# One list of work per engine and row, with the output projection split, in a cross-attention and mixture-of-experts kernel

## The reference

```python
x = x + attention(layernorm(x), ctx)      # x, ctx: 8 rows of the batch x 128 tokens x 256
x = x + moe(layernorm(x))

def attention(x, h_ctx_kv):               # 16 query heads, 4 key/value heads, width 128
    q = rms_norm(x @ wq, q_norm_w); k = rms_norm(x @ wk, k_norm_w); v = x @ wv
    k_ctx = rms_norm(h_ctx_kv @ wk_ctx, k_norm_w); v_ctx = h_ctx_kv @ wv_ctx
    q = q * cos + rotate_half(q) * sin;  k = k * cos + rotate_half(k) * sin
    # each key head serves 4 query heads: a group
    scores = q @ concat(k_ctx, k).T / sqrt(128) + causal mask on the second half
    out = softmax(scores) @ concat(v_ctx, v)
    return out.reshape(8, 128, 2048) @ wo

def moe(xt):                              # sigmoid router, best 2 of 8 experts, plus a shared expert
    ...
```

## Time and profile before

| | |
|---|---|
| median of 3 runs | 354.92 us (354.77 to 354.96) |
| the profiled execution | 355.51 us, of which span of the core 353.8 us |
| TensorE busy (PE) | 323.0 us, 91% |
| VectorE busy (DVE) | 313.5 us, 89% |
| ScalarE busy (ACT) | 260.5 us, 74% |
| GpSimd busy (POOL) | 170.0 us, 48% |
| granted TensorE clock | 0.999 of full speed |

### The profile page before, as it was taken

One profiled execution on the slowest core, in us unless ns is written; L12 is line 12 of the kernel. 1 busy time (PEld: TensorE's weight loads), 2 busy tenths in 40 slices (PEclk: granted clock), 3 DMA queues, 4 the chain that ended last, 5 costly groups with the idle time before them and its releaser, 6 DMA issues.

```text
span 353.8 us, 7342 instructions
## 1 busy us (share of the span) xinstructions
PE 323.0 (91%) x2242; PEld 218.4 (62%) x2242; DVE 313.5 (89%) x602; ACT 260.5 (74%) x910; POOL 170.0 (48%) x247
## 2 busy tenths in 40 slices
PE   6868878899999999999999999999999999999994
PEld 6444545476667666766676667666766677756452
DVE  1789999999999899989998999899989998866763
ACT  3786889766987698769866986798679756847641
POOL 4866648663754275428541744174417420072620
PEclk9999999999999999999999999999999999999999
DMA  7887200012034003500310002000100000055783
GB/s 235 318 265 238 48 0 0 3 30 17 1 114 98 11 0 110 109 4 0 59 44 0 0 0 44 0 0 0 30 0 0 3 2 0 2 99 99 131 156 111
DMA packets 42450, 21.07 MB, mean 60 GB/s; under 512 B 31672, under 2 KB 39872, under 8 KB 42432
## 3 DMA queue, kind: packets, MB, share of 16 engines
q1 hardware_dynamic: 41712, 20.60, 23.3%
q10 hardware_dynamic: 720, 0.26, 0.4%
HBM read 12.20 MB, written 1.05 MB: 37 GB/s over the span
## 4 chain that ended last, share of the span: by engine, by line
PE 35%; DVE 25%; ACT 19%; issue 11%; POOL 4%; DMA 3%; DVEq 1%; SPq 0%; ACTq 0%; POOLq 0%
PE proj L1400 10%; ACT probs L568 8%; DVE probs L1014 6%; PE pt_ps L1363 6%; DVE nmax L1002 4%; PE turn L1309 3%; PE o_ps L1373 3%; DVE pT_lo L940 3%; PE sc_ps L1330 3%; PE proj L1215 3%; ACT pT_hi L469 2%; POOL q_rot L799 2%; DVE q_t L931 2%; DMA wq<-in_L_xattn_wq_dram 2%; ACT q_junk L512 2%
## 5 line engine op out<-in xcount | busy, mean ns | idle before, releaser
L568 ACT ACTIVATE probs<-sc_ps,nbias,q_r 128x256 f32<-128x256 f32 x128 | 70.9, 571 | 4.3 <-DVE nbias L1006 3.8
L799 POOL TENSOR_TENSOR q_rot<-q_t 128x512 f32<-128x512 f32 x32 | 41.4, 1294 | 42.2 <-DVE q_t L933 41.4
L1014 DVE TENSOR_SCALAR probs<-probs,rden 128x256 f32<-128x256 f32 x128 | 51.8, 466 | 1.1
L512 ACT ACTIVATE q_junk<-proj 128x128 bf16<-128x128 f32 x128 | 34.1, 297 | 11.3 <-DVE q_t L933 11.2
L469 ACT ACTIVATE pT_hi<-pt_ps 128x512 f16<-128x512 f32 x64 | 34.8, 597 | 10.1 <-PE pt_ps L1363 10.1
L940 DVE SCALAR_TENSOR_TENSOR pT_lo<-pt_ps,pT_hi 128x512 f16<-128x512 f32 x64 | 41.0, 681 | 0.1
L1002 DVE TENSOR_REDUCE nmax<-sc_ps 128x4 f32<-128x1024 f32 x32 | 38.9, 1215 | 1.5 <-PE sc_ps L1352 1.5
L1215 PE MATMUL proj<-wq_hi,xT 128*128 128x512 f16 x128 | 38.1, 379 | 0.0
L1363 PE MATMUL pt_ps<-ident,probs 128*128 128x128 f32 x256 | 33.3, 273 | 0.8 <-DVE probs L1014 0.6
L753 POOL TENSOR_TENSOR q_r<-q_me,power 128x4 f32<-128x4 f32 x32 | 32.5, 1014 | 2.5
L469 ACT ACTIVATE qT_hi<-turn 128x512 f16<-128x512 f32 x32 | 19.4, 607 | 18.1 <-PE turn L1309 18.1
(11 more groups left out here) (216 smaller groups left out, 866.9 us busy)
## 6 DMA issues: line engine op xcount, KB each, us to landing
wq<-in_L_xattn_wq_dram SPq DMA_DIRECT2D x4, 512.0 KB, 7.6
w<-in_L_ffn_w_dram SPq DMA_DIRECT2D x2, 1024.0 KB, 11.0
wq<-in_L_xattn_wo_dram SPq DMA_DIRECT2D x1, 2048.0 KB, 8.2
ctx_b<-in_ctx_dram SPq DMA_DIRECT2D x8, 128.0 KB, 2.3
out_dram<-x_all SPq DMA_DIRECT2D x4, 256.0 KB, 2.2
x_all<-in_x_dram SPq DMA_DIRECT2D x1, 896.0 KB, 14.1
wkc<-in_L_xattn_wk_ctx_dram SPq DMA_DIRECT2D x1, 512.0 KB, 4.3
wk<-in_L_xattn_wk_dram SPq DMA_DIRECT2D x1, 512.0 KB, 5.2
```

The lines of the kernel that those rows point to most:

```text
L512: last = nc.scalar.activation(junk[:, head], bank[:, head], ACT.Square, scale=scale, accum_out=dst[:, h:h + 1])
L568: last = nc.scalar.activation(probs[:, h, :], sc_ps[:, h, :], ACT.Exp, bias=nbias[:, h:h + 1], scale=q_r[:, g, h:h + 1], accum_out=den[:, ...
L799: nc.gpsimd.tensor_tensor(q_rot[:], q_t1[:], q_t2[:], ALU.add).then_inc(q_added, 1)
L1014: last = nc.vector.tensor_scalar(probs[:, h, :], probs[:, h, :], rden[:, h:h + 1], None, ALU.mult)
```

## The change

The loops over `g` go. Each engine's `row` becomes a written list, and the orders are new:

- TensorE: in stage 0 the projection of group 2 stands behind the turn of group 1 and ahead of `turn_probs`. `out_proj` is split: groups 0 and 1 right after `scores(b, 1)` and ahead of the turn of group 2, groups 2 and 3 after the projection of group 3. The next row's group 0 is turned in stage 3, and `kc_turn` comes last.
- ScalarE: `p_copy` of a group ends its list rather than beginning the next one. The next row's `q_copy` of group 0 and `k_copy` come ahead of group 3's exponentials, `kc_copy` between their two halves (`exps` has a parameter `half`).
- VectorE: the maximum and `nbias` are two steps now (`scores_max`, `scores_bias`), and so are `rden` and the products with it (`sums`, `normalise` with a list of heads), with other work between the heads.
- POOL: `ln_root` stands first. Rows 1 to 6 are all written out, and the casts are eight pieces of half the size for each weight, spread over two rows. SyncE waits for these after rows 2, 4 and 6.
- `ctx_high` waits for `vc_proj` in row 1's case only. The last row and what follows it keep their steps.

The lists, in the order ScalarE, POOL, VectorE, TensorE. What stands under `if first:` and the lines that go are left out.

```diff
             def row(b, first, last):
+                u = G * b
+                exps(b, 0, 0)
+                exps(b, 0, 1)
+                if not first and not last:
+                    ctx_high(b + 1)
+                q_squares(b, 2)
+                if not first:
+                    o_copy(u - 1, 3)
+                vc_copy(b)
+                v_copy(b)
...
+                q_copy(b, 2)
+                if not last:
+                    ln_high(b + 1)
+                p_copy(u)
+                exps(b, 1, 0)
+                exps(b, 1, 1)
+                q_squares(b, 3)
+                o_copy(u, 0)
...
+                q_copy(b, 3)
+                p_copy(u + 1)
+                exps(b, 2, 0)
+                exps(b, 2, 1)
+                if not last:
+                    kc_squares(b + 1)
+                    q_squares(b + 1, 0)
+                    k_squares(b + 1)
+                o_copy(u + 1, 1)
+                if not last:
+                    kc_scale(b + 1)
+                if last:
+                    act.wait_ge(t_sh2, 1)
+                    copy(gateT[:].rearrange("p c e -> p (c e)"), proj[0][:, D:D + DC * E])
+                    copy(sh2T[:], proj[0][:, 0:D]).then_inc(r_sh2, 1)
+                    xn_copy(1)
...
+                p_copy(u + 2)
+                if not last:
+                    q_copy(b + 1, 0)
+                    k_copy(b + 1)
+                exps(b, 3, 0)
+                if not last:
+                    kc_copy(b + 1)
+                exps(b, 3, 1)
...
+                if not last:
+                    q_squares(b + 1, 1)
+                    q_copy(b + 1, 1)
+                    o_copy(u + 2, 2)
+                    p_copy(u + 3)
...
             def row(b, first, last, cast=None):
+                if not first and isinstance(b, int) and b == 1:
+                    wo_rest(1)
+                if cast:
+                    cast(0)
+                    cast(1)
+                if not last:
+                    ln_root(b + 1)
+                q_add(b, 2)
+                q_roots(b, 2)
+                if not last:
+                    ln_low(b + 1)
+                q_add(b, 3)
+                q_roots(b, 3)
...
+                if not first:
+                    l2_root(b - 1)
+                if cast:
+                    cast(2)
+                    cast(3)
+                if last:
+                    return
+                q_add(b + 1, 0)
+                kc_roots(b + 1)
+                k_roots(b + 1)
+                k_scale(b + 1)
+                q_roots(b + 1, 0)
...
+                q_add(b + 1, 1)
+                q_roots(b + 1, 1)
...
+            for b, start in ((1, 0), (2, 4)):
+                row(b, False, False, cast_to(w1_b, w1_32, d_w1, w1_cast, start))
+            for b, start in ((3, 0), (4, 4)):
+                row(b, False, False, cast_to(w3_b, w1_32, d_w3, w3_cast, start))
+            for b, start in ((5, 0), (6, 4)):
+                row(b, False, False, cast_to(w2_b, w2_32, d_w2, w2_cast, start))
...
+            def scores_bias(b, g):
+                u = G * b + g
                 dve.wait_ge(s_max, u + 1)
                 dve.wait_ge(q_root, u + 1)
                 seen(dve, s_exp, u)
                 nc.vector.tensor_tensor(nbias[:], nmax[:], q_r[:, g, :], ALU.mult).then_inc(s_bias, 1)
+            def sums(b, g):
                 u = G * b + g
                 dve.wait_ge(s_exp, u + 1)
                 nc.vector.reciprocal(rden[:], den[:]).then_inc(s_rden, 1)
+            def normalise(b, g, heads=range(R)):
+                dve.wait_ge(s_rden, G * b + g + 1)
+                for h in heads:
                     last = nc.vector.tensor_scalar(probs[:, h, :], probs[:, h, :], rden[:, h:h + 1], None, ALU.mult)
+                    if h == R - 1:
+                        last.then_inc(s_probs, 1)
...
             def row(b, first, last):
+                scores_max(b, 0)
...
+                q_low(b, 1)
+                if not first:
+                    o_low(u - 2, 2)
+                    scores_bias(b, 0)
+                    p_low(u - 1)
+                q_turn(b, 2)
+                sums(b, 0)
+                normalise(b, 0, (0,))
+                if not last:
+                    ln_stats(b + 1)
+                    dve.wait_ge(ln_stat, b + 2)
+                normalise(b, 0, (1,))
+                if not last:
+                    ln_gather(b + 1)
+                if not last and not first:
+                    ctx_low(b + 1)
+                normalise(b, 0, (2, 3))
+                vc_low(b)
+                v_low(b)
...
+                if not last:
+                    ln_scale(b + 1)
+                scores_max(b, 1)
+                scores_bias(b, 1)
+                q_low(b, 2)
+                if not first:
+                    o_low(u - 1, 3)
+                p_low(u)
+                q_turn(b, 3)
+                sums(b, 1)
+                normalise(b, 1, (0,))
+                if not first:
+                    residual(b - 1)
+                normalise(b, 1, (1, 2, 3))
...
+                o_low(u, 0)
+                scores_max(b, 2)
+                q_low(b, 3)
+                scores_bias(b, 2)
+                if not first:
+                    second_norm(b - 1)
+                p_low(u + 1)
+                if last:
+                    xn_copy(0)
+                else:
+                    q_turn(b + 1, 0)
+                sums(b, 2)
+                normalise(b, 2, (0,))
+                if not last:
+                    k_turn(b + 1)
+                normalise(b, 2, (1, 2, 3))
+                if not last:
+                    k_add(b + 1)
+                scores_max(b, 3)
+                o_low(u + 1, 1)
+                p_low(u + 2)
+                scores_bias(b, 3)
...
+                if not last:
+                    q_low(b + 1, 0)
+                    k_low(b + 1)
+                    q_turn(b + 1, 1)
+                    kc_low(b + 1)
+                sums(b, 3)
+                normalise(b, 3)
...
+                if last:
+                    o_low(u + 2, 2)
...
             def row(b, first, last):
+                scores(b, 0)
+                q_turn(b, 1)
...
+                q(b, 2)
+                if not first:
+                    turn_probs(u - 1)
+                vc(b)
...
+                v(b)
+                if not first:
+                    mix(u - 1, 3)
+                scores(b, 1)
+                if not first:
+                    out_proj(b - 1, (0, 1))
+                q_turn(b, 2)
+                turn_probs(u)
...
+                q(b, 3)
+                if not first:
+                    out_proj(b - 1, (2,))
+                    out_proj(b - 1, (3,))
+                mix(u, 0)
+                scores(b, 2)
+                q_turn(b, 3)
+                turn_probs(u + 1)
+                if not last:
+                    q(b + 1, 0)
+                    kc(b + 1)
+                    k(b + 1)
+                if last:
+                    turn_down_gate()
+                    turn_xn2(0, (q_sq, G * B))
+                    turn_xn2(1, (q_ready, G * B))
+                mix(u + 1, 1)
+                scores(b, 3)
+                turn_probs(u + 2)
+                if not last:
+                    q(b + 1, 1)
+                    q_turn(b + 1, 0)
+                    k_turn(b + 1)
+                if last:
+                    pe.wait_ge(r_sh2, 1)
+                    logits(0)
+                    turn_shared()
+                mix(u + 2, 2)
+                if not last:
+                    kc_turn(b + 1)
```

More of the change, by code:

```diff
@@ L557, in v_copy, with exps @@
                 copy(v_hi[:, 1, :], turn[:], V_SCALE / XW).then_inc(v_high, 1)
-            def exps(b, g, between=()):
+            def exps(b, g, half):
                 u = G * b + g
[L562 to L567, removed]
+                if half == 0:
+                    act.wait_ge(s_bias, u + 1)
+                    seen(act, p_turned, u)
+                for h in (2 * half, 2 * half + 1):
                     last = nc.scalar.activation(probs[:, h, :], sc_ps[:, h, :], ACT.Exp, bias=nbias[:, h:h + 1],
                                                 scale=q_r[:, g, h:h + 1], accum_out=den[:, h:h + 1])
-                    if h == R // 2 - 1:
-                        last.then_inc(s_exp_half, 1)
-                last.then_inc(s_exp, 1)
+                last.then_inc((s_exp_half, s_exp)[half], 1)
             def p_copy(u):
@@ L622, in _ @@
             wc_split(1)
+            q_copy(0, 1)
             def row(b, first, last):
[L625 to L640, removed]
-                        wo_split(3)
-                    if g == 0:
-                        v_copy(b)
-                    if (g or not first) and not (g == 3 and last):
-                        o_copy(u - 1, (g - 1) % G)
-                    if g == 2 and not last:
-                        kc_scale(b + 1)
-                        k_squares(b + 1)
```

(28 more changed lines are left out.)

225 lines of the change are left out of this document (63 added, 162 removed).

## The result

The changed kernel takes 362.1 us (median of 4 runs, 361.56 to 363.33), the kernel before 354.85 beside it. The ratio is 1.0216 (95% interval 1.0199 to 1.0233). Forecast were 359.9, slower, and a range of 352.0 to 363.0. The profiled execution of the changed kernel took 362.44, with a span of 360.7; the span of before was 353.8.

The account below looks back on a forecast made before the run. TensorE and VectorE, both nearly full, bound a middle row. Rows 0 and 1 at -1.2, rows 2 to 6 at +5.5 and row 7 at +0.7 sum to +5.0 on the 354.92 median: 359.9 us, range 352.0 to 363.0.

Parts of the forecast that it names:

- main case: First heads blocked by POOL's addition in stages 1 and 2, middle row 36.2 us, total 359.9; chance 0.55.
- rows 0 and 1: First two batch rows: row 0 gains 1.9 us, row 1 loses 0.7, together -1.2 (bounds -2.1 and +1.0).
- row 7: Last row: group 3's late bias delays its exponentials 1.2 us, partly covered by TensorE, +0.7 (bounds 0 and 1.2).
- the middle rows: Rows 2 to 6: each 36.2 us against 35.1, so 5 x 1.1 = +5.5 us.
- The stalls: VectorE's first-head normalisation in stages 1 and 2 held until POOL's addition ends, 1.06 us more each.
- Blocks don't happen: Rival: VectorE's first head starts before POOL's addition in stages 1 and 2; row closes at T+34.7, 350.9 us; chance 0.19.
- One block of two: Rival: stage 1 blocked, stage 2 free, about 35.4 us a row, 355.1 us, no change; chance 0.09.
- the last `wo_split` (1.14): Row 0, VectorE: this split now follows all the next scores need, so row 1's T comes about 61.1 to 61.6.
- TensorE has output products to cover 0.5 of it: Row 7: output products hide 0.5 us of the exponentials' 1.2 us delay, leaving +0.7.
- The late bias: Stage 3, VectorE: group 3's bias comes only after `o_low` 0.6 and `p_low` 1.2, at T+31.5; named a cost.
- two copies ahead: Stage 3: group 3's first exponentials now have two copies ahead; argument against the rival that TensorE alone decides, chance 0.08.
- the chain through the context keys: Stage 3: `kc` turns behind the mix, its copy ends T+33.85, the last two exponentials release readers at T+35.1.

Follow-up runs that it names:

- both heads free: Changed kernel with VectorE's residual (stage 1) and key rotation (stage 2) moved ahead of all four normalisations: 353.20 us, ratio 0.9967 to the kernel before.
- stage 1 free: Changed kernel with only the residual moved ahead of the normalisations of group 1: 357.98 us, ratio 1.0110 to the kernel before.
- late splits: Changed kernel with two of row 0's output weight splits (VectorE's first, ScalarE's third) moved behind work for the next row's scores: 360.59 us, ratio 1.0166.
- idle products: Changed kernel with 24 idle TensorE products ahead of row 0's second key turn and 16 behind it: 361.82 us, ratio 1.0203 to the kernel before.

## Why the forecast was right, and which terms were off

The forecast of slower, and of why, held. The measured 362.1 us lies 2.2 above the 359.9 and just outside the main case's own 357 to 362: rows 0 and 1 and row 7 were forecast 2.6 too low together, the middle rows 0.7 too high.

**The row was right step by step.** With T = 208.55, the turn of group 1 in row 5, and the rows shown above or beside them in the same timeline:

| step | forecast | measured |
|---|---|---|
| turn of group 2 | T+10.65 | T+10.65 |
| maximum of group 2 | T+19.65 | T+19.52 |
| wait of TensorE for the probabilities | 0.9 | 0.72 |
| `k_turn` | T+30.9 | T+30.70 |
| bias of group 3 | T+31.5 | T+31.29 |
| first two exponentials end | T+33.15 | T+32.99 |
| second pair of scores | T+35.1 | T+34.96 |
| turn of group 1, next row | T+36.2 | T+36.07 |

The 0.13 a row that were missing make up the difference of 5.5 and 4.8, with five rows. The stalls were there in stage 1 of rows 1 to 7 and in stage 2 of rows 0 to 6: 14 single heads of over 1.2 us in the whole trace, none in the kernel with both heads free.

**The price of what the rivals described was met too.** "Blocks don't happen" named a row of 34.7 us and 350.9 in all; with both blocks taken away the row is 34.78. The time was 353.2 and not 350.9: the rival put -2.7 on rows 0 and 1, and the trace with both heads free shows -1.1 there (98.63 against 99.77 at the first maximum of row 2), with -1.6 in the five middle rows and +0.8 from row 7 on. "One block of two" named stage 1 as the blocked one, at 35.4 a row; that kernel has 34.91, and 35.53 belongs to the other, with stage 2 blocked.

**Rows 0 and 1 was the term that failed** (-1.2 forecast, +0.8 measured, and +1.5 counted from row 0's first maximum, 73.85 against 72.37). The step reads "the last `wo_split` (1.14) now stands behind all that the next scores need. So T of row 1 comes at about 61.1 to 61.6". T came at 63.62. One split stood behind; the other, `wo_split(0)`, stood ahead of `q_low(1, 0)`, and ScalarE's `wo_split(2)` ahead of `p_copy`. With both moved T came at 61.24, in the range that the forecast gave, although row 0's first maximum was 0.9 later in that execution. VectorE's maximum of row 1 came only 2.6 us behind it, though, where the forecast had 1 us, so even then rows 0 and 1 took 71.78 us from row 0's first maximum, against 72.37 before: -0.6 and not -1.2. The other part of the miss, 1.0 us at T and 0.3 to 0.9 at the end of row 1, is the clock in those executions in which it fell; the forecast had no term for it. Two slips in this term are small: the maximum of row 1 came at 64.09 in the trace of before (64.16 is where the window was cut), and from 35.62 to 36.2 is +0.6, not +0.7.

**Row 7 was mis-sized** (+0.7 forecast, +1.3 measured). The step was that "TensorE has output products to cover 0.5 of it". It covers none: the early bias gave back the whole 1.26 us at the reciprocal, and it is still there at the router's last `weight`. The 1.3 itself is a sum in which two things left out nearly cancel. From the last maximum to the reciprocal it is 1.49 longer than before, and the stretch ahead of that maximum 0.48 longer (25.31 us against 24.83; 24.69 with stage 1 free). The stretch behind the last `weight` was 0.67 shorter, since the execution of before had the long form of it (25.86).

**A cost that was named but wasn't the limit.** Here the forecast was partly lucky. The late bias and "two copies ahead" of the exponentials stand in the trace where the forecast put them, yet taking them away gave nothing in a middle row. The sum came out right since the chain through the context keys (turn behind the mix, copy, last exponentials) was in it as well and ends at the same time.

## What to carry to other kernels

When one engine's elementwise instruction is slow only beside another engine's, put an instruction that reads PSUM into that place before moving anything else: here it turned a loss of 7 us into a gain of 1. Work that seems free to move may be the cover of a wait, so look for what the next instruction waits on. Write the edges of a loop (first and last row) out as carefully as its middle, since two splits of row 0 and one bias of row 7 were worth 2.9 us here (350.78 against 353.20, surplus -3.9 against -1.0).

## What was not expected of the hardware

- A stalled head ends with POOL's addition, however late it began. Starting 0.04 us after the addition it took 1.38 us, starting 0.32 after it 1.10; both end 0.15 us after the addition. Three heads after it take 0.85. The Trainium skill (VectorE: DVE Perf Modes, Mode 2×_2P) says that a single-source instruction with source and destination in SBUF can use both read ports and double its rate, and that a PSUM source can't. The trace agrees on which kind stood still, the heads and not the instructions with a PSUM operand. It doesn't show a doubled rate: a head of 256 elements takes 0.35 us alone, the residual of 256 elements with an operand in PSUM 0.42.
- A two-operand instruction on SBUF loses too: in the kernel with late splits, the 128x1024 `wo_lo` that began 0.53 us into an addition took 1.83 us, and 1.22 when POOL was quiet:

```profile
59.16 1.27 POOL L811 TENSOR_TENSOR q_rot<-q_t 128x512 f32<-128x512 f32 x1
59.69 1.83 DVE L957 SCALAR_TENSOR_TENSOR wo_lo<-wq,wo_hi 128x1024 f16<-128x1024 f32 x1
...
62.69 1.22 DVE L957 SCALAR_TENSOR_TENSOR wo_lo<-wq,wo_hi 128x1024 f16<-128x1024 f32 x1
```

- The granted clock fell in the middle of a kernel that was 90% busy on TensorE, after one sparse stretch (1.29 us busy of 3.50), and not in every execution: it fell in three of six traces that share that stretch. While it was down, a low product of the scores and its mask took 0.32 us from start to start (62.34, 62.66) and 0.16 at full clock (61.99, 62.16 in the kernel with idle products).
